# Mixer B's decays in chunks of 64 tokens, two heads stacked on the partitions

## The reference

```python
        proj = hidden_states @ in_proj_w * _mup_vector()
        ...
        xBC = jax.nn.silu(jnp.swapaxes(conv + conv_b[None, :, None], 1, 2))
        x = xBC[..., :INTER].reshape(b, l, G, HPG, PDIM)
        Bm = xBC[..., INTER:INTER + GTS].reshape(b, l, G, NSTATE)
        Cm = xBC[..., INTER + GTS:].reshape(b, l, G, NSTATE)
        dt = jax.nn.softplus(dt + dt_bias)
        A = -jnp.exp(A_log)
        dA = jnp.exp(dt * A).reshape(b, l, G, HPG)
        dtx = dt.reshape(b, l, G, HPG)[..., None] * x
        def step(state, inp):
            dA_t, dtx_t, B_t, C_t = inp
            state = state * dA_t[..., None, None] + jnp.einsum('bgcp,bgn->bgcpn', dtx_t, B_t)
            y_t = jnp.einsum('bgn,bgcpn->bgcp', C_t, state)
            return (state, y_t)
        ...
        y = y + D.reshape(1, 1, G, HPG, 1) * x
        ...
        out = yn * jax.nn.silu(z)
        return out @ out_proj_w
```

## Time and profile before

| | us |
|---|---|
| median of 3 runs (lowest, highest) | 2777.86 (2776.61, 2777.88) |
| the profiled execution: its own time | 2777.8 |
| its span, first to last instruction | 2776.1 |
| PE busy | 2685.3 (97%) |
| DVE busy | 1967.5 (71%) |
| ACT busy | 1530.3 (55%) |
| POOL busy | 904.9 (33%) |

### The profile page before, as it was taken

How to read it: one execution, slowest core, us unless ns; L and a number is a source line. 1 busy time by engine, 2 the same in 40 slices (tenths; PEclk the granted TensorE clock), 3 DMA queues, 4 the chain that set the end, 5 groups by cost and what they waited for, 6 DMA issues and landing times. The chain is left out here.

```text
span 2776.1 us, 49901 instructions
## 1 busy us (share of the span) xinstructions
PE 2685.3 (97%) x17452; PEld 1843.6 (66%) x17452; DVE 1967.5 (71%) x3701; ACT 1530.3 (55%) x2450; POOL 904.9 (33%) x611
## 2 busy tenths in 40 slices
PE   8999999999999998999899999999999999997998
PEld 7777777777777775456766667766677666673454
DVE  5666666666666655396788888888888888886377
ACT  3444444454445443342576677666777767765332
POOL 2222222233222223142233443334333344323144
PEclk8999999999999999999999999999999999998999
DMA  4000000000001005245000000000000000012433
GB/s 129 24 23 23 23 23 23 23 23 23 26 26 30 15 25 217 85 165 198 12 24 23 23 19 19 23 23 22 8 23 23 23 23 23 8 36 114 156 129 137
DMA packets 79994, 139.57 MB, mean 50 GB/s; under 512 B 17958, under 2 KB 17958, under 8 KB 78892
## 3 DMA queue, kind: packets, MB, share of 16 engines
q1 hardware_dynamic: 70812, 125.92, 13.0%
q10 hardware_dynamic: 9104, 12.63, 1.3%
HBM read 104.98 MB, written 33.55 MB: 50 GB/s over the span
## 5 line engine op out<-in xcount | busy, mean ns | idle before, releaser
L725 PE MATMUL work<-b_xnT,shared_w 128*128 128x256 f32 x2304 | 534.1, 387 | 3.5 <-DVE b_parts L1348 2.5
L725 PE MATMUL work<-a_xnT,shared_w 128*128 128x256 f32 x2176 | 498.1, 386 | 1.3
L725 PEld LDWEIGHTS work<-b_xnT,shared_w 128*128 128x128 f32 x2304 | 431.6, 192 | 79.1 <-issue 17.0
L725 PEld LDWEIGHTS work<-a_xnT,shared_w 128*128 128x128 f32 x2176 | 410.9, 192 | 70.6 <-issue 12.3
L1388 DVE TENSOR_TENSOR b_decay<-b_decay,b_gt 128x1024 f32<-128x1024 f32 x256 | 349.1, 1395 | 72.5 <-ACT b_decay L1034 71.9
L1027 ACT ACTIVATE b_decay<-seg 128x1024 f32<-128x1024 f32 x256 | 252.2, 1025 | 192.7 <-PE seg L867 184.8
L1617 POOL TENSOR_TENSOR b_rhs<-b_l_side,of_head 128x1024 fp32r<-128x1024 f32 x32 | 97.9, 3060 | 590.6 <-DVE b_l_side L1357 590.6
L1034 ACT ACTIVATE b_decay<-b_decay 128x1024 f32<-128x1024 f32 x256 | 263.6, 1066 | 0.0
L1652 POOL TENSOR_TENSOR a_y<-a_y,a_skip 128x1024 f32<-128x1024 f32 x32 | 90.0, 2812 | 473.7 <-DVE a_y L1377 473.7
L824 PE MATMUL work<-a_w_out,a_yz 128*128 128x512 f32 x512 | 229.4, 601 | 3.4 <-DVE a_y L1377 3.4
L1267 DVE SCALAR_TENSOR_TENSOR shared_cv<-shared_pre,a_conv_w,shared_cv 128x256 f32<-128x256 f32 x432 | 189.7, 482 | 60.3 <-ACT shared_cv L969 54.6
(11 more groups left out here) (328 smaller groups left out, 4572.9 us busy)
## 6 DMA issues: line engine op xcount, KB each, us to landing
shared_x<-in_L_attn_a_x SPq DMA_DIRECT2D x16, 512.0 KB, 3.5
a_x_res<-in_L_attn_a_x SPq DMA_DIRECT2D x32, 256.0 KB, 2.6
x_mid<-a_x_res SPq DMA_DIRECT2D x32, 256.0 KB, 2.0
shared_w<-in_L_ffn_d_w SPq DMA_DIRECT2D x2, 4096.0 KB, 13.5
f_d_w<-in_L_ffn_d_w SPq DMA_DIRECT2D x2, 4096.0 KB, 16.8
f_x_res<-x_mid SPq DMA_DIRECT2D x8, 1024.0 KB, 5.7
f_bc_w<-x_mid SPq DMA_DIRECT2D x8, 1024.0 KB, 5.5
shared_x<-x_mid SPq DMA_DIRECT2D x16, 512.0 KB, 4.1
```

The costliest lines, as they stand in the source:

```text
L725: mm = nc.tensor.matmul(dst, w_in[:, k, col:col + m], xnT[:, k, :], start=(k == 0), stop=(k == KD - 1))
```

## The change

For mixer B alone (`PAIRED`), a tile's 128 tokens s are cut into two chunks c of 64, and two heads are stacked on the 128 partitions. Chunk 0 has 128 columns (all tokens l), chunk 1 has 64 (the tokens of its own chunk). The block with s in chunk 1 and l in chunk 0 is not computed. A slot of 8 heads is then 4 pairs x 192 = 768 columns instead of 1024. `xdt` becomes block diagonal, [two heads x 64 tokens, 2 x 16 columns], with a block for each chunk. What goes with it:

- a segment unit is eight products (four of 256 columns, four of 128) instead of four of 512; PE's first unit of a supertile also waits for tile 0's x by dt
- a diagonal slot is still eight products, four of 128 and four of 64 columns
- B times C is made in 64-wide strips, eight products instead of two for a supertile
- `make_xdt` is four instructions of 64 partitions for a tile; for tile 0 it reads x from PSUM (`seg[0]`)
- `lhs` is made by two instructions instead of one; both `rhs` have 512 columns instead of 1024
- POOL makes `dte` = dt times the decay once in a supertile and `b_xw` from x and `dte` in one instruction; it no longer waits for `xdt`. Eleven small instructions prepare masks and columns at the stage's start
- ACT's first copy of x waits for `b_xw` of the supertile before

```diff
-    PADDED = HP < 32
+    PAIRED = HP < 32
...
+    HALF = P // 2
+
+    WIDE = P + HALF if PAIRED else P
+    SLOT = 4 * WIDE if PAIRED else 8 * P
...
-        lhs, rhs = sb("lhs", [P, 2, P], F32R), [sb(f"rhs{k}", [P, 8, P], F32R) for k in range(2)]
+        RHS = 4 if PAIRED else 8
+        lhs = sb("lhs", [P, NSET, 2, P], F32R) if PAIRED else sb("lhs", [P, NSET, P], F32R)
+        rhs = [sb(f"rhs{k}", [P, RHS, P], F32R) for k in range(NSET)]
...
-        xdt = sb("xdt", [P, 2, H // 2, 48]) if PADDED else sb("xdt", [P, 2, H, HP])
+        xdt = sb("xdt", [P, 2, 2, H // 2, 32]) if PAIRED else sb("xdt", [P, 2, H, HP])
+        dte = sb("dte", [P, 2, H]) if PAIRED else None
...
-        decay = sb("decay", [P, DECAYS, 8, P])
+        decay = sb("decay", [P, DECAYS, SLOT])
...
+        def pair_half(p, k):
+            return (p + k) % 2
...
                 def b_times_c(bank):
+                    if PAIRED:
+
+                        for j in range(2):
+                            first, second = (slice(j * P + c * HALF, j * P + (c + 1) * HALF) for c in range(2))
+                            for o in range(2):
+                                rows = slice(o * HALF, (o + 1) * HALF)
+                                nc.tensor.matmul(bank[rows, j * WIDE:j * WIDE + P], bcs[0:N, 0, first],
+                                                 bcs[0:N, 1, j * P:(j + 1) * P], start=True, stop=True)
+                            for o in range(2):
+                                rows = slice(o * HALF, (o + 1) * HALF)
+                                mm = nc.tensor.matmul(bank[rows, j * WIDE + P:(j + 1) * WIDE], bcs[0:N, 0, second],
+                                                      bcs[0:N, 1, second], start=True, stop=True)
+                        return mm
                     for j in range(2):
                         mm = nc.tensor.matmul(bank[:, GCOL + j * P:GCOL + (j + 1) * P], bcs[0:N, 0, j * P:(j + 1) * P],
...
                     pe.wait_ge(seg_taken, FREE + tile * NS + 2 * p)
                     if xt_last is not None:
                         pe.wait_ge(xt_ready, FREE + 4 * xt_last + 4)
+                        if PAIRED:
+                            pe.wait_ge(xdt_done, FREE + 2 * xt_last + 1)
+                    if PAIRED:
+
+                        for c in range(2):
+                            cols, past = slice(c * P, c * HALF + P), slice(c * HALF, P)
+                            for k in range(4):
+                                r, first = 32 * k, 2 * pair_half(p, k)
+                                mm = nc.tensor.matmul(
+                                    x_bank(k)[:, 0:2 * WIDE].rearrange("p (e l) -> p e l", e=2)[:, :, cols],
+                                    lhs[r:r + 32, p // 2, c, :], rhs[p // 2][r:r + 32, first:first + 2, past],
+                                    start=True, stop=True)
+                                if c == 1 and k % 2 == 1:
+                                    mm.then_inc(seg_full, 1)
+                        return
...
                 def ydiag_slot(tile, j, s):
                     pe.wait_ge(m_ready, FREE + tile * NS + s + 1)
-                    if PADDED:
-
-                        for e in range(2):
-                            slot, odd, _ = unit_bank(s // 2, 2 * (s % 2) + e)
-                            for q in range(4):
-                                mm = nc.tensor.matmul(ybank[32 * q:32 * q + 32, slot * P:(slot + 1) * P],
-                                                      xdt[:, j, 4 * slot + q, 16 * odd:16 * odd + 32],
-                                                      decay[:, slot_buffer(j, s), 4 * e + q, :],
-                                                      start=False, stop=True, skip_group_check=True)
+                    d = decay[:, slot_buffer(j, s)]
+                    if PAIRED:
+
+                        for c in range(2):
+                            for e in range(2):
+                                k = 2 * (s % 2) + e
+                                slot = unit_bank(s // 2, k)[0]
+                                for pair in range(2):
+                                    q = 2 * pair_half(s // 2, k) + pair
+                                    at = (2 * e + pair) * WIDE
+                                    mm = nc.tensor.matmul(ybank[32 * q:32 * q + 32, slot * P + c * HALF:(slot + 1) * P],
+                                                          xdt[:, j, c, 4 * slot + q, :],
+                                                          d[:, at + c * P:at + P + c * HALF],
+                                                          start=False, stop=True, skip_group_check=True)
...
                         act.wait_ge(xdt_done, FREE + 2 * sec.i)
+                        if PAIRED:
+                            act.wait_ge(xw_ready, FREE + 2 * sec.i)
...
                     act.wait_ge(ydiag_done, FREE + 2 + tile * NS + s - 3)
-                    nc.scalar.activation(decay[:, slot_buffer(j, s)].rearrange("p h l -> p (h l)"),
-                                         seg[s % 2][:, :], ACT.Relu, scale=-1.0).then_inc(seg_taken, 1)
+                    d, src = decay[:, slot_buffer(j, s)], seg[s % 2][:, :]
+                    if PAIRED:
+                        d = d.rearrange("p (h l) -> p h l", h=2)
+                        src = src.rearrange("p (h l) -> p h l", h=2)[:, :, 0:2 * WIDE]
...
                 def dt_finish(sec):
                     dve.wait_ge(sp_ready, sec.n + 1)
+                    if PAIRED:
+                        dve.wait_ge(dte_ready, FREE + sec.n)
...
                     i = sec.i
                     if j == 0:
                         dve.wait_ge(ydiag_done, FREE + 2 + 2 * i * NS)
-                        dve.wait_ge(xw_ready, FREE + 2 * i)
-                    dve.wait_ge(xt_ready, FREE + 4 * i + 2 * j + 2)
-                    if PADDED:
-                        xt4 = xt[:, j, :].rearrange("p (h o q) -> p h o q", o=2, q=HP)
+                        if not PAIRED:
+                            dve.wait_ge(xw_ready, FREE + 2 * i)
+                    if PAIRED:
+
+                        dve.wait_ge(xt_ready, FREE + 4 * i + 2 * j + 2)
+                        xt4 = (xt[:, j, :] if j else seg[0][:, :]).rearrange("p (h o q) -> p h o q", o=2, q=HP)
                         dt4 = dt[:, j, :].rearrange("p (h o) -> p h o", o=2)
-                        for odd in range(2):
-                            ins = nc.vector.tensor_tensor(xdt[:, j, :, 32 * odd:32 * odd + HP], xt4[:, :, odd, :],
-                                                          dt4[:, :, odd:odd + 1].to_broadcast([P, H // 2, HP]),
-                                                          ALU.mult)
+                        for o in range(2):
+                            for c in range(2):
+                                tokens = slice(c * HALF, (c + 1) * HALF)
+                                ins = nc.vector.tensor_tensor(
+                                    xdt[o * HALF:(o + 1) * HALF, j, c, :, HP * o:HP * o + HP], xt4[tokens, :, o, :],
+                                    dt4[tokens, :, o:o + 1].to_broadcast([HALF, H // 2, HP]), ALU.mult)
                         ins.then_inc(xdt_done, 1)
                     else:
...
                     nc.vector.tensor_scalar(flat[1], flat[0], c["l_row"][0:R], c["s_row"][0:R], ALU.mult, ALU.add
                                             ).then_inc(l_side_ready, 1)
-                    nc.vector.tensor_scalar(lhs[0:R, 0:NSET, :].rearrange("p k l -> p (k l)"), flat[0],
-                                            c["s_row"][0:R], c["l_row"][0:R], ALU.mult, ALU.add).then_inc(lhs_ready, 1)
+                    if PAIRED:
+
+                        by_chunk = parts[:].rearrange("p k (c s) -> p k c s", c=2)
+                        for o in range(2):
+                            ins = nc.vector.tensor_scalar(lhs[:, :, :, o * HALF:(o + 1) * HALF], by_chunk,
+                                                          s_side[:, o:o + 1], l_rows[:, o:o + 1], ALU.mult, ALU.add)
+                        ins.then_inc(lhs_ready, 1)
+                    else:
+                        nc.vector.tensor_scalar(lhs[0:R, 0:NSET, :].rearrange("p k l -> p (k l)"), flat[0],
...
                     dve.wait_ge(l_side_ready, tile + 1)
-                    nc.vector.tensor_tensor(rhs[0][0:R], l_side[0:R, 0].unsqueeze(1).to_broadcast([R, 8, P]),
-                                            c["of_head"][0:R].unsqueeze(2).to_broadcast([R, 8, P]), ALU.mult
+                    of = of_pair if PAIRED else c["of_head"]
+                    nc.vector.tensor_tensor(rhs[0][0:R], l_side[0:R, 0].unsqueeze(1).to_broadcast([R, RHS, P]),
+                                            of[0:R].unsqueeze(2).to_broadcast([R, RHS, P]), ALU.mult
                                             ).then_inc(rhs_ready[0], 1)
...
-                    d = decay[:, slot_buffer(j, s)]
```

(32 more changed lines are left out.)

35 lines of the change are left out of this document (32 added, 3 removed).

## The result

The changed kernel takes 2814.3 us (median of 4 runs, 2812.3 to 2817.6), the kernel before 2777.2 (2775.9 to 2777.9). The ratio is 1.0136, 95% interval 1.0121 to 1.0151: 37 us slower. The forecast was 2807, slower, by a stall of PE in each supertile. The profiled execution took 2817.6 us (span 2815.8), 39.8 more than that of before.

The account below looks back on a forecast made before the run. PE was taken to bound mixer B (76.57 of 76.80 us busy). Stall +2.8, clock +1.3, diagonal -1.7 and segment units -0.3 gave +2.1 in 14 supertiles: 2777.8 + 29 = 2807 us, range 2744 to 2840.

Parts of the forecast that it names:

- Columns on PE: Mixer B's diagonal blocks and segment products on PE: fewer columns save 27.6 us a stage and 0.05 us a segment unit.
- D: Rival, diagonal blocks on PE: narrow bursts take as long as wide ones, 2835 us; chance 0.06.
- E: Rival, diagonal blocks on PE: a burst is paced by its records one after the other, 2829 us; chance 0.04.
- B times C: PE, ahead of the products with the state: +0.2 us a supertile, hidden by 0.28 us of waiting for DVE.
- Turns: Two-input instructions of DVE and POOL alternate, one of each; 11.7 us to out_add's end, DVE 3.3 us late.
- C: Rival, x by dt of the second tile: DVE isn't held, all saved columns count, 2744 or 2747 us; chance 0.23.
- F: Rival, DVE: half-partition instructions at half price, DVE 2.2 us late, PE's stall 1.3, no low clock, 2774 us; chance 0.05.
- PE's stall: PE stands 2.4 us before small1, waiting for DVE's out_add; the first block starts 2.8 us later in all.
- The clock: After PE's gap the granted clock falls and blocks run at half speed: 1.3 us a supertile, bounds 0 and 4.
- B: Rival, PE before small1: the stall without the low clock, +11 us, 2789 us; chance 0.12.
- The sum: Per middle supertile: +2.8 stall, +1.3 clock, -1.7 diagonal, -0.3 segment units, making +2.1; over 14 supertiles +29 us.

## Why the prediction held, point by point

- **Columns on PE.** Diagonal 1.46 us for four slots, forecast 1.46; segment unit 0.38, forecast 0.38. Narrow bursts follow their columns down to 64, so D and E fall, and with E the 25 ns of the Trainium skill ("TensorE: Matmul & The Clock Gate", section "Wait — 56ns, not 53.3ns?") as a floor across strips: a burst of four records of 64 columns takes (1.46 - 8 x 0.118) / 8 = 65 ns, 16 a record, if the wide bursts keep their 118. Without that assumption, 64 records in 1.46 us are 22.8 ns each in the mean, already under 25.
- **B times C.** Its own size was right (0.65 us forecast, +0.2; measured +0.19). But I had it hidden under the wait for `b_rs`, at no cost, and this step failed: the knot starts 8.95 us after the transposes of x instead of 8.46. I had looked at PE's wait, not at what ends it. DVE copies `b_rs` behind `gt` and x by dt of tile 0, and B times C makes `gt` later and wider, so the cover moves too. Of the 0.5 us, 0.28 stands on PE ahead of the products with the state (5.60 us from the transposes to the first of them, 5.32 before, and just so in the two runs with `b_rs` ahead), and 0.26 is the longer wait for `b_rs`: with the copy ahead a supertile gives back 0.54 us in the changed kernel and 0.28 in the kernel before. Of the 0.28, 0.19 is in B times C; the other 0.1 is just ahead of it (0.54 us from BT's start to its own instead of 0.44), for a reason that no run looked for. The books close: the periods 76.52 and 74.74 are 1.78 apart, the 2.0 to 2.1 of the columns less 0.28.
- **Turns.** 11.42 us from the knot to the end of out_add, forecast 11.7. The splitting alone brings it about, the place alone undoes it, and the order of starting alone undoes it. C and F fall: DVE is held, and 64 partitions cost 0.686 us like 128, not 0.6, and far from half.
- **PE's stall.** 2.08 us before small1, forecast 2.4. The first block starts 23.04 us after the transposes, 19.88 before: +3.16, of which 0.5 from the head and 2.67 from DVE, forecast 2.8 from DVE alone. Some 0.3 of it is not ahead of small1 but ahead of the first block, which waits for `b_parts` (2.07 us from dt to the block instead of 1.74).
- **The clock.** This term was mis-sized: 2.2 us in the mean, forecast 1.3, inside its bounds of 0 and 4. I had reckoned half speed on the blocks alone and wrote that dt loses nothing. Every second time the low stretch begins in dt (granted clock 0.62 from 1832.47 to 1835.17, 2.90 us instead of 1.90), and the blocks behind it take 6.04 us. B falls.
- **The sum.** In a middle supertile +0.5 head, +2.7 stall, +2.2 clock, -1.7 and -0.3 columns: +3.4, forecast +2.1. From the first small1 of mid-stage to the last, 13 periods, it is +42.3 us, 3.25 each. Ahead of them the run is 1.8 us shorter and behind them 0.7, which makes the 39.8 between the two profiled executions. Of the 1.8 some 1.4 is there already at the end of mixer A, which the change doesn't touch. So the forecast came nearer in total (2807 against 2814.3) than in its terms: both misses, head and clock, went the same way, 1.3 us a supertile, and a part of them was taken back by these 2.5 us and by medians that lie under the profiled executions.

## What to carry to other kernels

Before an elementwise instruction on SBUF is split, look at what the other elementwise engine does at the same time: each piece may wait for one whole instruction over there, as long as there is one, so the price goes by the number of pieces and the length of the neighbour's instructions, not by the bytes. Then try the same pieces where the neighbour is idle, or let the neighbour start later by one wait. A change that saves work on the bounding engine and yet loses is worth a second look at the order: here the same arithmetic, in two orders, stands at 1.4% slower and 1.4% faster than before.

## What the runs showed of the hardware

- 64 partitions cost VectorE as much as 128: 0.686 us in both cases for 512 columns. I had taken 0.6 from the price by columns.
- A gap of 1.19 us of TensorE was already followed by a clock of 1.2 GHz in 2 of 13 cases, one of 1.63 in 11 of 13, one of 2.51 in only 10 of 13. Its price came in two sizes, 1.4 and 2.95 us in turn. No low stretch followed 13 gaps of 0.76 us. What decides between the cases wasn't found.
- Keeping TensorE busy with repeated work in a stall that can't be removed gave back 29 of 37 us (2814.3 to 2785.6).
